# Three states of h instead of two, shorter rings for B and the scan inputs, and takes three slots behind the products

## The chip, the cores and the metric

The kernel runs on one core of one Trainium2 chip. The metric is the time of the slowest core in microseconds (us); with one core that is simply the time of the program on the device. The median of three runs before the change is 8832.22 us.

## The reference

The input x has 8192 rows of 512 numbers. The program computes x = x + layernorm(mamba(layernorm(x))) and then x = x + layernorm(soft mixture of experts(layernorm(x))). All of it is float32. The change lies in the mamba part, which has two layers and reads, cut to what matters:

```python
xc, z = split(x @ W_in.T)                 # 1024 channels each
u = silu(causal_conv4(xc) + b_c)
dt, B, C = split(u @ W_x.T)               # 32, 16 and 16 columns
delta = softplus(dt @ W_dt.T + b_dt)
h[t] = exp(delta[t] * A) * h[t-1] + delta[t] * B[t] * u[t]     # per channel and each of 16 states
y = sum over states of h * C + u * D
out = (y * silu(z)) @ W_out.T
```

The recurrence over t runs for 1024 channels times 16 states over 8192 rows, in each of two layers.

## The kernel before

**Tiling.** Each layer is cut into 16 chunks of T = 512 rows, so there are 32 chunks in all, numbered G. Channels lie on the 128 partitions, in NB = 8 blocks. A chunk has GROUPS = 32 groups, k = 0 to 31: one of the two halves of the blocks (HB = 4 blocks) with one of the 16 states. A group is four scans, one for each block of the half. So a chunk is SLOTS_BODY = 128 slots, slot s = 4k + b. All engines walk through the same 128 slots, each in an instruction stream that is written out in full, and semaphores tie them together.

**What each engine does in a slot.**

- ScalarE (ACT) computes the decay exp(delta * A) of the slot into PSUM (`decay_of`, L747). There are four such buffers, one bank each, so ACT runs at most four slots ahead of the scans.
- GpSimd (POOL) computes the inputs of two scans at once, w * B with w = delta * u, in one instruction for a pair of slots (`inputs`, L952). It reads a row of B repeated over all partitions (`b_rep`, loaded by SyncE, `load_b`, L404). `b_rep` has four rows and `bu` has four pairs. POOL also adds softplus parts, forms w, and adds pairs of products (`W_AT`, `SUM_AT`), 24 more instructions of the same size in a chunk.
- VectorE (DVE) runs the scan (`scan`, L1028) into `h[:, k % 2, b, :]`. After it DVE takes the transposed state of the group before, multiplies it by C and adds it up (`add_state`, L1048). Three of four such tiles fall to DVE and one to ACT (`product`, L763). In slots 4 and 5 of each eight no add falls to DVE.
- TensorE (PE) transposes the state of the group before, one tile j of 128 rows in each slot (`turn_states`, L538): tile (k-1, j) stands in slot 4k + j + 1, so tile (k-1, 3) stands in the first slot of group k+1. The transposes go to two PSUM banks in turn (`turn_bank`). Behind its tile PE does the slot's share of the projections (L467, L513), whose results go to a ring of two PSUM banks, `proj`. Skip tiles (u * D, L546, slots 4 to 7 and 30 to 39) and y tiles (L554, slots 22 to 28 and 116 to 122) come on top of the state tiles.

**The order of the projections** is written out by `timetable()`. It walks through `ORDER` (conv_half, conv, out, x_proj, turn_c, delta and gate tiles), gives each slot about equal PE work (`WORK`), and puts the moment when ACT takes a finished tile out of its bank TAKE_LAG = 4 slots behind the tile's last product (`TAKE`). A conv tile may start CONV_LAG slots behind its conv_half tile, and turn_c XDBL_LAG slots behind x_proj. The silu of u and of z runs over a whole half (128x2048) behind the last take of the half. It needs another table of functions than exp, so there is a table load ahead of it and one behind it. `silu_at` moves a silu further back when it would fall just ahead of ACT's products.

**The waits around the change.** A scan of the first slot of group k waits until tile (k-2, 3) has been transposed and until `h_last` of group k-2 has been saved, since it overwrites that state. `load_b` for group k waits until the inputs of group k-4 are made. `inputs` for slots s and s+1 waits until scan s-5 is done (`s - 6 + C_SCAN`).

Of the kernel before, what the change touches and what calls it, by code (L numbers as in the profile page):

```python
# [5 lines left out]
ALU = mybir.AluOpType  # L6
# [4 lines left out]
P = 128  # L11
# [7 lines left out]
T = 512  # L19
# [27 lines left out]
PRODUCTS = {"delta": 1, "conv_half": KD, "conv": TAPS, "out": NB, "x_proj": NB, "delta_next": 1, "turn_c": 1, "gate": KD}  # L47
SLOTS_BODY = GROUPS * HB
PAIRS = SLOTS_BODY // 2
TAKE_LAG, TAPS_LEAD, XDBL_LAG, CONV_LAG, PROD_LAG = 4, 2, 4, 4, 2  # L50

W_AT = {17: ("sum", 2), 21: ("product", 2), 25: ("sum", 3), 29: ("product", 3),
        49: ("sum_next", 0), 53: ("product_next", 0), 57: ("sum_next", 1), 61: ("product_next", 1)}
# [35 lines left out]
WEIGHT = {"x_proj": 1.1, "delta": 1.25, "delta_next": 1.25, "turn_c": 0.5, "state": 0.55, "skip": 1.05, "y": 0.55}  # L89

def silu_at(end):
    at = end + TAKE_LAG
    behind = (at - PROD_LAG - 5) % (2 * J)
    return at if behind < 5 else at + 2 * J - behind


def timetable():
    room = [-sum(WEIGHT[tile[0]] for tile in tiles_at) for tiles_at in TURN_AT]  # L100
    whole = sum(PRODUCTS[kind] * WEIGHT.get(kind, 1.0) for kind, _, _ in ORDER) - sum(room)
    room = [r + whole / (SLOTS_BODY - 3) for r in room]
    slot, left, end_of = 0, room[0], {}
    work, take = [[] for _ in range(SLOTS_BODY)], [[] for _ in range(2 * SLOTS_BODY)]
    for i, (kind, x, earliest) in enumerate(ORDER):
        if kind == "conv":
            earliest = end_of["conv_half", x] + CONV_LAG
        if kind == "x_proj":
            earliest = silu_at(end_of["conv", NB - 1]) + 1
# [12 lines left out]
        end = end_of[kind, x] = slots[-1]  # L122
        if kind == "conv_half":
            take[end + TAKE_LAG - TAPS_LEAD].append(("taps", x, i))
        take[end + TAKE_LAG].append((kind, x, i))
        if kind.startswith("delta") and x % 2 == 1:
            for q, part in enumerate(("exp", "ln")):
                take[end + TAKE_LAG + 1 + q].append((part + kind[5:], x // 2, i))
        if kind == "conv" and x % HB == HB - 1:
            take[silu_at(end)].append(("silu_u", x // HB, i))  # L130
        if kind == "gate" and x % HB == HB - 1:
            take[silu_at(end)].append(("silu_z", x // HB, i))
    return work, take, end_of


# [80 lines left out]
C_SCAN, C_HS, C_BU, C_XC, C_Z, C_Y, C_W, C_PROJ, C_TURN, C_PROD, C_DEC = 8, 2, PAIRS, NB, 2, NB, NB, 8, 8, 8, SLOTS_BODY  # L216


class Kind:
# [52 lines left out]
def mamba_stack(nc, ctx, d):  # L272
    def sb(name, shape):
        return ctx.enter_context(nc.sbuf_tensor(name, shape, F32))

    def ps(name, shape):
        return ctx.enter_context(nc.psum_tensor(name, shape, F32))

    def sem(name):
        return ctx.enter_context(nc.semaphore(name))  # L280
# [19 lines left out]
    xdbl = sb("xdbl", [P, T])  # L300
    c_next = sb("c_next", [P, J, STATES])
    c_now = sb("c_now", [P, J, STATES])
    b_rep = sb("b_rep", [P, 4, T])
    bu = sb("bu", [P, 4, 2, T])
    h = sb("h", [P, 2, HB, T])
    h_last = sb("h_last", [P, GROUPS * HB])
    prod = sb("prod", [P, 3, 2, HB * P])
    acc = sb("acc", [P, 2, J, HB * P])
    stage = sb("stage", [P, T])
    spare = sb("spare_m", [P, 1])  # L310

    decay = ps("decay", [P, HB, T])
    turn = ps("turn", [P, TURNS, T])
    proj = ps("proj", [P, RING, T])

# [6 lines left out]
    out_weights_in = sem("out_weights_in")  # L322
    xconv_in = sem("xconv_in")
    xgate_in = sem("xgate_in")
    brep_in = [sem(f"brep_in{r}") for r in range(4)]
    b_stored = sem("b_stored")
    out_stored = sem("out_stored")
    ident_set = sem("ident_set")
# [29 lines left out]
    def _(sp):  # L358
# [38 lines left out]

        def load_b(G, k):

            sp.wait_ge(bu_set, G * PAIRS + (2 * (k - 4) + 2 + C_BU))  # L400
            if k == 0:
                sp.wait_ge(b_stored, G * 16 + 32)
            src = d["b_rows"][bass.ds(G, 1), k % STATES, :].rearrange("a t -> (a t)").partition_broadcast(P)
            sp.dma_start(b_rep[:, k % 4, :], src).then_inc(brep_in[k % 4], 16)  # L404

        def body(G, kind, before_last=False):
            new = kind.layer + 1
# [52 lines left out]
    def _(pe):  # L460
# [72 lines left out]
        def turn_states(out, G, k, j):  # L533

            if j == 0:
                pe.wait_ge(scanned, G * SLOTS_BODY + (HB * k + HB + C_SCAN))
            for b in range(HB):
                mm = pe.transpose(out[:, b * P:(b + 1) * P], h[:, k % 2, b, j * P:(j + 1) * P], ident[:])  # L538
            mm.then_inc(turn_full, 1)

        def skip(out, G, layer, hf, j):
# [85 lines left out]
    def _(act):  # L627
# [113 lines left out]
        def decay_of(G, kind, k, b):  # L741
            hf, n = divmod(k, STATES)
            blk, s = hf * HB + b, HB * k + b
            act.wait_ge(scanned, G * SLOTS_BODY + (s + 1 - HB + C_SCAN))
            if n == 0:
                act.wait_ge(delta_set, G * HB + (blk // 2 + 1))
            act.activation(decay[:, b, :], delta[:, blk, :], ACT.Exp,  # L747
                           scale=neg_a[:, n, blk:blk + 1]).then_inc(decay_set, 1)

        def product(G, kind, tile):  # L750
# [26 lines left out]
        def save_last(G, k):  # L777

            act.wait_ge(scanned, G * SLOTS_BODY + (HB * k + HB + C_SCAN))
            act.copy(h_last[:, HB * k:HB * k + HB], h[:, k % 2, :, T - 1]).then_inc(hlast_set, 1)  # L780

        exp_tables()
        X, n = 0, 0
# [128 lines left out]
    def _(pool):  # L912
# [30 lines left out]
        def inputs(G, k, pr):  # L943

            hf, n = divmod(k, STATES)
            blk, s = hf * HB + 2 * pr, HB * k + 2 * pr
            if pr == 0:
                pool.wait_ge(brep_in[k % 4], G * (GROUPS * 4) + (k // 4 + 1) * 16)
# [3 lines left out]
            pool.tensor_tensor(bu[:, s // 2 % 4, :, :], w[:, blk:blk + 2, :],  # L952
                               b_rep[:, k % 4, :].unsqueeze(1).to_broadcast([P, 2, T]), ALU.mult).then_inc(bu_set, 1)

        def scaled(G, kind, tile, carried):
            turns, base = kind.turns, act_base(G, kind)
# [55 lines left out]
    def _(dve):  # L1012
# [4 lines left out]
        def scan(G, kind, k, b):  # L1017
            s = HB * k + b
            dve.wait_ge(decay_set, G * SLOTS_BODY + (s + 1))
            dve.wait_ge(bu_set, G * PAIRS + (s // 2 + 1 + C_BU))  # L1020
            if b == 0:

                dve.wait_ge(hlast_set, G * GROUPS + (k - 2 + 1 + C_HS))
                tile = "state", (k - 2) % GROUPS, J - 1
                if tile in kind.turns.index:
                    dve.wait_ge(turn_full, turn_base(G, kind) + (kind.turns.index[tile] + 1))
            start = zeros[:, 0:1] if kind.first or kind.enters else h_last[:, s:s + 1]
            dve.tensor_tensor_scan(h[:, k % 2, b, :], decay[:, b, :], bu[:, s // 2 % 4, b % 2, :], start,  # L1028
                                   ALU.mult, ALU.add).then_inc(scanned, 1)

        def add_state(G, kind, k, j):
# [890 lines left out]
```

## Time and profile before

| | |
|---|---|
| median of three runs | 8832.22 us (8822.1 to 8835.82) |
| the profiled execution's own time | 8832.35 us |
| span of its trace | 8829.7 us |
| mean granted TensorE clock | 0.928 |
| PE busy | 7621.7 us, 86% |
| DVE busy | 7550.2 us, 86% |
| POOL busy | 6729.4 us, 76% |
| ACT busy | 5909.6 us, 67% |

The scans run from 242 us to about 7970 us of the span. What is before is the input norm and the first chunk's projections, what is behind is the mixture of experts. The page's chain of work that ended last lies in the last stage only, so for the mamba stage one reads which wait ends last on the busiest engine. Matmul ends are modelled, so PE's busy time is not its limit by itself.

### The profile page before, as it was taken

The numbers are of one execution on the slowest core, as the hardware profiler recorded it, in microseconds if no ns is written. First come the engines' busy times: TensorE is split into PE (matmuls) and PEld (weight loads), VectorE is DVE, ScalarE is ACT, GpSimd is POOL, SyncE is SP. The second block draws the span as 40 slices with busy tenths as digits, with TensorE's granted clock in tenths as the row PEclk, the third lists the DMA queues.
The fourth block names the chain that finished last, engine by engine and source line by source line (L and its number), as shares of the span: only waits on it lengthen the run. The fifth ranks groups of instructions, "written<-read, shape, count | busy, mean of one in ns | idle before, by whom it ended". The sixth has DMA issues, their size and how long they took to land. (4 is left out here: it accounts for less than half of the span.)

```text
span 8829.7 us, 103475 instructions
## 1 busy us (share of the span) xinstructions
PE 7621.7 (86%) x31688; PEld 4308.0 (49%) x31688; DVE 7550.2 (86%) x8674; ACT 5909.6 (67%) x10830; POOL 6729.4 (76%) x2890
## 2 busy tenths in 40 slices
PE   5788888888889888888888888888888888876886
PEld 3444454444444444444444444444444444445753
DVE  2899999999999999999999999999999999995717
ACT  5777777677677777766777777777766776754515
POOL 0888888888888888888888888888888888881203
PEclk7899999999999999999999999999999999977789
DMA  5111111111111111121111111111111111113434
GB/s 192 49 50 48 44 48 50 49 50 50 50 46 50 48 50 44 48 60 59 60 50 50 44 52 50 50 48 44 48 50 50 50 50 50 41 43 136 176 117 152
DMA packets 223325, 550.37 MB, mean 62 GB/s; under 512 B 26272, under 2 KB 26528, under 8 KB 201824
## 3 DMA queue, kind: packets, MB, share of 16 engines
q1 hardware_dynamic: 196448, 459.30, 16.6%
q10 hardware_dynamic: 26368, 84.95, 2.4%
q8 instruction: 239, 3.92, 0.2%
q14 instruction: 270, 2.21, 0.1%
HBM read 442.44 MB, written 101.71 MB: 62 GB/s over the span
## 5 line engine op out<-in xcount | busy, mean ns | idle before, releaser
L952 POOL TENSOR_TENSOR bu<-w,b_rep 128x1024 f32<-128x1024 f32 x2048 | 4822.4, 2361 | 1160.1 <-DVE h L1028 1157.6
L1028 DVE TENSOR_TENSOR_SCAN h<-decay,h_last,bu 128x512 f32<-128x512 f32 x3840 | 4810.5, 1273 | 340.9 <-PE turn L538 271.5
L747 ACT ACTIVATE decay<-delta,neg_a 128x512 f32<-128x512 f32 x4096 | 2804.8, 690 | 1377.1 <-DVE h L1028 1309.7
L538 PEld LDWEIGHTS turn<-ident_m,h 128*128 128x128 f32 x16384 | 1997.2, 146 | 2987.5 <-DVE acc L1048 1582.8
L538 PE MATMUL turn<-ident_m,h 128*128 128x128 f32 x16384 | 2665.0, 288 | 635.3 <-DVE acc L1048 502.2
L1048 DVE SCALAR_TENSOR_TENSOR acc<-turn,c_now,acc 128x512 f32<-128x512 f32 x3072 | 2240.2, 729 | 190.6 <-PE turn L538 188.8
L763 ACT ACTIVATE prod<-turn,c_now 128x512 f32<-128x512 f32 x1024 | 701.6, 685 | 675.3 <-PE turn L538 674.5
L467 PE MATMUL proj<-zy,w_out 128*128 128x512 f32 x2048 | 1123.6, 654 | 19.9 <-ACT delta L714 19.0
L467 PE MATMUL proj<-conv_in,conv_diag 128*128 128x512 f32 x2048 | 1047.7, 608 | 71.0 <-ACT halo L681 71.0
L967 POOL TENSOR_TENSOR prod<-prod 128x1024 f32<-128x1024 f32 x448 | 1056.0, 2357 | 14.7 <-ACT prod L763 14.7
L467 PE MATMUL proj<-x_gate,w_in 128*128 128x512 f32 x2048 | 1054.1, 619 | 0.0
L467 PE MATMUL proj<-x_conv,w_in 128*128 128x512 f32 x2048 | 1018.8, 596 | 20.7 <-DMA x_conv<-xt 17.4
L467 PEld LDWEIGHTS proj<-zy,w_out 128*128 128x128 f32 x2048 | 371.5, 213 | 206.0 <-issue 169.4
L1028 DVE TENSOR_TENSOR_SCAN h<-decay,zeros_m,bu 128x512 f32<-128x512 f32 x256 | 320.1, 1272 | 145.2 <-POOL bu L952 123.1
L467 PEld LDWEIGHTS proj<-conv_in,conv_diag 128*128 128x128 f32 x2048 | 333.3, 194 | 217.3 <-issue 113.2
L467 PEld LDWEIGHTS proj<-x_gate,w_in 128*128 128x128 f32 x2048 | 347.2, 200 | 140.6 <-issue 140.6
L467 PEld LDWEIGHTS proj<-x_conv,w_in 128*128 128x128 f32 x2048 | 332.4, 191 | 166.1 <-issue 154.5
L934 POOL TENSOR_TENSOR delta<-delta,w 128x1024 f32<-128x1024 f32 x128 | 302.0, 2359 | 92.9 <-ACT w L722 92.9
L513 PE MATMUL proj<-xdbl,w_dt 65*128 65x512 f32 x512 | 297.3, 665 | 75.5 <-ACT stage L737 75.1
L546 PE MATMUL turn<-d_diag,u 128*128 128x128 f32 x2048 | 293.3, 287 | 67.2 <-DVE acc L1048 51.6
L673 ACT ACTIVATE conv_diag<-ident_m,par 128x128 f32<-128x128 f32 x1024 | 325.1, 392 | 3.6 <-DMA par<-in_par_dram 3.6
L546 PEld LDWEIGHTS turn<-d_diag,u 128*128 128x128 f32 x2048 | 251.9, 194 | 106.6 <-DVE acc L1048 73.2
(170 smaller groups left out, 5911.5 us busy)
## 6 DMA issues: line engine op xcount, KB each, us to landing
b_rep<-b_rows SPq DMA_DIRECT2D x1024, 256.0 KB, 3.2
x_conv<-xt SPq DMA_DIRECT2D x32, 1024.0 KB, 6.9
x_gate<-xt SPq DMA_DIRECT2D x32, 1024.0 KB, 4.8
xt<-stage ACTq DMA_DIRECT2D x128, 256.0 KB, 3.3
x_n<-in_x_dram SPq DMA_DIRECT2D x16, 1024.0 KB, 5.6
xt<-xt_n ACTq DMA_DIRECT2D x16, 1024.0 KB, 4.3
x_l<-in_x_dram SPq DMA_DIRECT2D x16, 1024.0 KB, 6.1
mt_l<-xt SPq DMA_DIRECT2D x16, 1024.0 KB, 6.1
```

The costliest lines, as they stand in the source:

```text
L467: mm = pe.matmul(out[0:lhs.shape[1], :], lhs, rhs, start=n == 0, stop=n == count - 1)
L513: pe.matmul(out, w_dt[:, b * P:(b + 1) * P], xdbl[0:XD + 1, :], start=True, stop=True).then_inc(proj_full, 1)
L538: mm = pe.transpose(out[:, b * P:(b + 1) * P], h[:, k % 2, b, j * P:(j + 1) * P], ident[:])
L546: mm = pe.matmul(out[:, b * P:(b + 1) * P], u[:, hf * HB + b, j * P:(j + 1) * P], d_diag[:, hf * HB + b, :], start=True, stop=True)
L673: act.activation(conv_diag[:, b % 2, k, :], ident[:], ACT.Copy, scale=par[:, STATES + k, b:b + 1])
L747: act.activation(decay[:, b, :], delta[:, blk, :], ACT.Exp, scale=neg_a[:, n, blk:blk + 1]).then_inc(decay_set, 1)
L763: act.activation(prod[:, V_BUFFER[q], k % 2, :], turn[:, BANK[tile], :], ACT.Copy, scale=c_now[:, j, n:n + 1]).then_inc(v_done, 1)
L934: pool.tensor_tensor(delta[:, lo:lo + 2, :], delta[:, lo:lo + 2, :], w[:, lo:lo + 2, :], ALU.add).then_inc(delta_set, 1)
L952: pool.tensor_tensor(bu[:, s // 2 % 4, :, :], w[:, blk:blk + 2, :], b_rep[:, k % 4, :].unsqueeze(1).to_broadcast([P, 2, T]), ALU.mult).the ...
L967: pool.tensor_tensor(total, total, prod[:, V_BUFFER[q]], ALU.add).then_inc(vsum_set, 1)
L1028: dve.tensor_tensor_scan(h[:, k % 2, b, :], decay[:, b, :], bu[:, s // 2 % 4, b % 2, :], start, ALU.mult, ALU.add).then_inc(scanned, 1)
L1048: dve.scalar_tensor_tensor(out, src, scalar, out, ALU.mult, ALU.add).then_inc(x_done, 1)
```

## The change

The state h gets three buffers, the rows of B two, the scan inputs three pairs. All the rings now run on over the chunks (group or slot number modulo the ring's length). The three lags of the timetable go from 4 to 3 and `silu_at` is dropped, so a silu follows the take of its last tile directly. The memory used stays the same: h grows by 8 KB in each partition, b_rep and bu shrink by 4 KB each. Worked out from the timetable, in slots: silu of u moves from 42 to 41 and from 65 to 64, silu of z from 119 to 114 and from 130 to 128 (that is slot 2 and slot 0 of the next chunk). The projections behind x_proj start one slot earlier (77 instead of 78), and their takes come two slots earlier in places: the take of the second out tile moves from slot 87 to 85, of the third from 95 to 93.

```diff
-TAKE_LAG, TAPS_LEAD, XDBL_LAG, CONV_LAG, PROD_LAG = 4, 2, 4, 4, 2
+TAKE_LAG, TAPS_LEAD, XDBL_LAG, CONV_LAG, PROD_LAG = 3, 2, 3, 3, 2
+H_RING = 3
+B_RING = 2
+DEC_RING = 4
+BU_RING = 3
-def silu_at(end):
-    at = end + TAKE_LAG
-    behind = (at - PROD_LAG - 5) % (2 * J)
-    return at if behind < 5 else at + 2 * J - behind
...
-            take[silu_at(end)].append(("silu_u", x // HB, i))
+            take[end + TAKE_LAG].append(("silu_u", x // HB, i))
...
-            take[silu_at(end)].append(("silu_z", x // HB, i))
+            take[end + TAKE_LAG].append(("silu_z", x // HB, i))
...
-    b_rep = sb("b_rep", [P, 4, T])
-    bu = sb("bu", [P, 4, 2, T])
-    h = sb("h", [P, 2, HB, T])
+    b_rep = sb("b_rep", [P, B_RING, T])
+    bu = sb("bu", [P, BU_RING, 2, T])
+    h = sb("h", [P, H_RING, HB, T])
...
-            sp.wait_ge(bu_set, G * PAIRS + (2 * (k - 4) + 2 + C_BU))
+            n = G * GROUPS + k
+            sp.wait_ge(bu_set, G * PAIRS + (2 * (k - B_RING) + 2 + C_BU))
...
-            pool.wait_ge(scanned, G * SLOTS_BODY + (s - 6 + C_SCAN))
+            pool.wait_ge(scanned, G * SLOTS_BODY + (s + 2 - 2 * BU_RING + C_SCAN))
...
-                dve.wait_ge(hlast_set, G * GROUPS + (k - 2 + 1 + C_HS))
-                tile = "state", (k - 2) % GROUPS, J - 1
-                if tile in kind.turns.index:
-                    dve.wait_ge(turn_full, turn_base(G, kind) + (kind.turns.index[tile] + 1))
+                dve.wait_ge(hlast_set, G * GROUPS + (k - H_RING + 1 + C_HS))
+                old = "state", (k - H_RING) % GROUPS, J - 1
+                if k >= H_RING or old in CARRIED and not kind.first:
+                    dve.wait_ge(turn_full, turn_base(G, kind) + (kind.turns.index[old] + 1))
+                elif not kind.first:
+                    dve.wait_ge(turn_full, turn_base(G, kind) + (ALL_TURNS.index[old] + 1 - TURN_TILES))
```

The other lines replace `k % 2`, `k % 4` and the like by the running numbers modulo the new lengths.

## Rows read from the trace of the kernel before

**Rows 1.** Timeline of SyncE's queue (start us, length us, what): loads of x_gate.

```profile
2179.17 0.33 SPq L391 DMA_DIRECT2D x_gate<-xt  x1
...
2421.52 0.33 SPq L391 DMA_DIRECT2D x_gate<-xt  x1
```

**Rows 2.** Waits of DVE, 200 to 8000 us: total us, times, longest.

```profile
DVE h L1028 <- PE turn L538: 287.8, 278, 3.1
DVE acc L1048 <- PE turn L538: 188.8, 189, 3.4
DVE zy L1057 <- ACT zy L731: 128.2, 32, 4.0
...
DVE h L1028 <- ACT decay L747: 73.6, 93, 1.3
```

**Rows 3.** Busy by stretch (PE, PEld, DVE, ACT, POOL; clock): tenth chunk, five stretches.

```profile
2419.40:2661.75 242.35, 215.76 (x900) 118.56 (x900) 220.41 (x233) 171.14 (x318) 205.46 (x89) 0.95 0.15 49
2465.36:2468.77 3.41, 3.41 (x8) 1.68 (x7) 2.68 (x3) 2.38 (x4) 3.41 (x2) 0.50 0.22 76
2557.51:2560.93 3.42, 3.09 (x13) 2.95 (x14) 3.42 (x4) 3.02 (x7) 3.42 (x2) 0.50 0.11 32
2574.58:2577.99 3.41, 3.41 (x8) 1.58 (x7) 2.73 (x3) 3.41 (x8) 2.15 (x1) 0.50 0.48 154
2591.65:2598.48 6.83, 6.20 (x12) 2.82 (x11) 2.85 (x4) 5.42 (x9) 6.35 (x3) 0.50 0.26 76
2639.43:2646.26 6.83, 5.75 (x16) 3.58 (x17) 5.29 (x6) 4.21 (x8) 4.46 (x2) 0.50 0.07 17
```

**Rows 4.** Timelines of PE and DVE, slots 85 to 96: idle time in brackets.

```profile
2573.83 1.37 PE L513 MATMUL proj<-xdbl,w_dt 65*128 65x512 f32 x2 [1.25 <-ACT stage L737]
...
2590.23 1.12 PE L513 MATMUL proj<-xdbl,w_dt 65*128 65x512 f32 x2 [1.25 <-ACT stage L737]
...
2576.09 0.75 DVE L1048 SCALAR_TENSOR_TENSOR acc<-turn,c_now,acc 128x512 f32<-128x512 f32 x1 [0.68 <-PE turn L538]
...
2579.45 0.75 DVE L1048 SCALAR_TENSOR_TENSOR acc<-turn,c_now,acc 128x512 f32<-128x512 f32 x1 [1.42 <-PE turn L538]
...
2595.40 0.75 DVE L1048 SCALAR_TENSOR_TENSOR acc<-turn,c_now,acc 128x512 f32<-128x512 f32 x1 [1.61 <-PE turn L538]
2599.26 1.28 DVE L1028 TENSOR_TENSOR_SCAN h<-decay,h_last,bu 128x512 f32<-128x512 f32 x1 [3.11 <-PE turn L538]
```

**Rows 5.** Timelines of ACT and DVE, slots 116 to 120: the silu of z.

```profile
2635.29 1.28 ACT L731 ACT_TABLE_LOAD   x1
2636.58 1.91 ACT L731 ACTIVATE zy<-zy 128x2048 f32<-128x2048 f32 x1
...
2638.59 0.69 DVE L1057 TENSOR_TENSOR zy<-turn,zy 128x512 f32<-128x512 f32 x1 [4.01 <-ACT zy L731]
...
2647.21 1.28 DVE L1028 TENSOR_TENSOR_SCAN h<-decay,h_last,bu 128x512 f32<-128x512 f32 x1 [2.48 <-PE turn L538]
```

**Rows 6.** Timelines of ACT and DVE, slots 40 to 43: first silu of u.

```profile
2492.04 0.71 ACT L747 ACTIVATE decay<-delta,neg_a 128x512 f32<-128x512 f32 x1
...
2500.65 1.30 ACT L747 ACTIVATE decay<-delta,neg_a 128x512 f32<-128x512 f32 x2
...
2494.49 1.28 DVE L1028 TENSOR_TENSOR_SCAN h<-decay,h_last,bu 128x512 f32<-128x512 f32 x1 [0.85 <-ACT decay L747]
...
2501.38 1.28 DVE L1028 TENSOR_TENSOR_SCAN h<-decay,h_last,bu 128x512 f32<-128x512 f32 x1 [1.29 <-ACT decay L747]
```

**Rows 7.** POOL from slot 97 on, DVE at slot 114, and b_rep's issues.

```profile
2602.53 2.36 POOL L952 TENSOR_TENSOR bu<-w,b_rep 128x1024 f32<-128x1024 f32 x1 [3.99 <-DVE h L1028]
...
2621.39 7.01 POOL L952 TENSOR_TENSOR bu<-w,b_rep 128x1024 f32<-128x1024 f32 x3
...
2629.64 1.28 DVE L1028 TENSOR_TENSOR_SCAN h<-decay,h_last,bu 128x512 f32<-128x512 f32 x1
...
DMA to landing us min/median/max: 3.0/3.2/10.0
```

More of the change, by code:

```diff
@@ L108, in timetable @@
         if kind == "x_proj":
-            earliest = silu_at(end_of["conv", NB - 1]) + 1
+            earliest = end_of["conv", NB - 1] + TAKE_LAG + 1
         if kind in ("turn_c", "delta_next"):
@@ L215 @@
 TURN_TILES, TURN_FIRST = len(ALL_TURNS.order), len(FIRST_TURNS.order)
-C_SCAN, C_HS, C_BU, C_XC, C_Z, C_Y, C_W, C_PROJ, C_TURN, C_PROD, C_DEC = 8, 2, PAIRS, NB, 2, NB, NB, 8, 8, 8, SLOTS_BODY
+C_SCAN, C_HS, C_BU, C_XC, C_Z, C_Y, C_W, C_PROJ, C_TURN, C_PROD, C_DEC = 8, H_RING, PAIRS, NB, 2, NB, NB, 8, 8, 8, SLOTS_BODY
 class Kind:
@@ L310, in mamba_stack @@
     spare = sb("spare_m", [P, 1])
-    decay = ps("decay", [P, HB, T])
+    decay = ps("decay", [P, DEC_RING, T])
     turn = ps("turn", [P, TURNS, T])
@@ L324, in mamba_stack @@
     xgate_in = sem("xgate_in")
-    brep_in = [sem(f"brep_in{r}") for r in range(4)]
+    brep_in = [sem(f"brep_in{r}") for r in range(B_RING)]
     b_stored = sem("b_stored")
@@ L403, in load_b @@
             src = d["b_rows"][bass.ds(G, 1), k % STATES, :].rearrange("a t -> (a t)").partition_broadcast(P)
[L404 removed]
+            sp.dma_start(b_rep[:, n % B_RING, :], src).then_inc(brep_in[n % B_RING], 16)
         def body(G, kind, before_last=False):
@@ L537, in turn_states @@
             for b in range(HB):
-                mm = pe.transpose(out[:, b * P:(b + 1) * P], h[:, k % 2, b, j * P:(j + 1) * P], ident[:])
+                mm = pe.transpose(out[:, b * P:(b + 1) * P], h[:, (G * GROUPS + k) % H_RING, b, j * P:(j + 1) * P], ident[:])
             mm.then_inc(turn_full, 1)
@@ L743, in decay_of @@
             blk, s = hf * HB + b, HB * k + b
-            act.wait_ge(scanned, G * SLOTS_BODY + (s + 1 - HB + C_SCAN))
+            act.wait_ge(scanned, G * SLOTS_BODY + (s + 1 - DEC_RING + C_SCAN))
             if n == 0:
                 act.wait_ge(delta_set, G * HB + (blk // 2 + 1))
-            act.activation(decay[:, b, :], delta[:, blk, :], ACT.Exp,
+            act.activation(decay[:, (G * SLOTS_BODY + s) % DEC_RING, :], delta[:, blk, :], ACT.Exp,
                            scale=neg_a[:, n, blk:blk + 1]).then_inc(decay_set, 1)
@@ L779, in save_last @@
             act.wait_ge(scanned, G * SLOTS_BODY + (HB * k + HB + C_SCAN))
-            act.copy(h_last[:, HB * k:HB * k + HB], h[:, k % 2, :, T - 1]).then_inc(hlast_set, 1)
+            act.copy(h_last[:, HB * k:HB * k + HB], h[:, (G * GROUPS + k) % H_RING, :, T - 1]).then_inc(hlast_set, 1)
         exp_tables()
@@ L945, in inputs @@
             hf, n = divmod(k, STATES)
-            blk, s = hf * HB + 2 * pr, HB * k + 2 * pr
+            blk, s, g = hf * HB + 2 * pr, HB * k + 2 * pr, G * GROUPS + k
             if pr == 0:
-                pool.wait_ge(brep_in[k % 4], G * (GROUPS * 4) + (k // 4 + 1) * 16)
+                pool.wait_ge(brep_in[g % B_RING], (g // B_RING + 1) * 16)
             if n == 0:
                 pool.wait_ge(w_set, G * NB + (blk + 2 + C_W))
-            pool.wait_ge(scanned, G * SLOTS_BODY + (s - 6 + C_SCAN))
-            pool.tensor_tensor(bu[:, s // 2 % 4, :, :], w[:, blk:blk + 2, :],
-                               b_rep[:, k % 4, :].unsqueeze(1).to_broadcast([P, 2, T]), ALU.mult).then_inc(bu_set, 1)
+            pool.wait_ge(scanned, G * SLOTS_BODY + (s + 2 - 2 * BU_RING + C_SCAN))
+            pool.tensor_tensor(bu[:, (G * PAIRS + s // 2) % BU_RING, :, :], w[:, blk:blk + 2, :],
+                               b_rep[:, g % B_RING, :].unsqueeze(1).to_broadcast([P, 2, T]), ALU.mult).then_inc(bu_set, 1)
         def scaled(G, kind, tile, carried):
@@ L1021, in scan @@
             if b == 0:
-                dve.wait_ge(hlast_set, G * GROUPS + (k - 2 + 1 + C_HS))
-                tile = "state", (k - 2) % GROUPS, J - 1
-                if tile in kind.turns.index:
-                    dve.wait_ge(turn_full, turn_base(G, kind) + (kind.turns.index[tile] + 1))
+                dve.wait_ge(hlast_set, G * GROUPS + (k - H_RING + 1 + C_HS))
[4 more added lines that the diff above has]
+                    dve.wait_ge(turn_full, turn_base(G, kind) + (ALL_TURNS.index[old] + 1 - TURN_TILES))
             start = zeros[:, 0:1] if kind.first or kind.enters else h_last[:, s:s + 1]
-            dve.tensor_tensor_scan(h[:, k % 2, b, :], decay[:, b, :], bu[:, s // 2 % 4, b % 2, :], start,
+            dve.tensor_tensor_scan(h[:, (G * GROUPS + k) % H_RING, b, :], decay[:, (G * SLOTS_BODY + s) % DEC_RING, :], bu[:, (G * PAIRS + s // 2) % BU_RING, b % 2, :], start,
                                    ALU.mult, ALU.add).then_inc(scanned, 1)
```

## The prediction

> **What bounds the kernel now.** I read first the page's busy shares: PE and DVE are level, so neither is plainly the bound and the mamba stage has to be read by its waits. Then the repeat: SyncE's load of x_gate comes at 2179.17 and again one chunk later at 2421.52 [rows 1], so a chunk takes 242.35 us, and nearly all chunks repeat it closely. In one chunk DVE works 220.41 us, PE 215.76, POOL 205.46, ACT 171.14 [rows 3]. DVE has the most work and stands idle for 21.9 us of 242.35. A stage in which DVE never waited would take 220.4 us a chunk; everything I can win lies in those 21.9 us. Over the stage DVE's waits [rows 2] are 287.8 (scan behind a transpose), 188.8 (add behind a transpose), 128.2 (gating behind the silu of z) and 73.6 (scan behind a decay): 678.4 us in all, 21.2 for each of 32 chunks. (POOL's wait for the first chunk's inputs is not counted, the change doesn't touch it.)
>
> The reader should then see where in the chunk these waits sit, since they are few and large, and that they have causes two steps back. In slots 85 and 92 PE stands 1.25 us because ACT has not yet taken an out tile out of the two-bank ring; right behind it DVE waits 0.68 and 1.42, and 1.61 and 3.11 [rows 4]. The granted clock shows why the second numbers are larger than 1.25: it is 0.50, that is 1.2 GHz, in 2574.58 to 2577.99 and in 2591.65 to 2598.48, just behind the two stands of PE, and 2.4 GHz between [rows 3]. At slot 116 DVE waits 4.01 us for the silu of z, PE stands with it, the clock is at 1.2 GHz from 2639.43 to 2646.26, and DVE waits another 2.48 at slot 120 [rows 3, 5]. So a late take or a late silu is paid twice, once as the wait and once as the slow clock behind it. Five stretches of 23.9 us together are at the low clock in each chunk, PE busy in 21.9 of them [rows 3]: at the high clock that work would be about 10.9 us shorter, PE's work then 204.8 us a chunk. PE has room in 229 us, but not much.
>
> **Three states of h.** The scan of a group's first slot no longer waits for the transpose that PE does in the same slot; the tile it now waits for lies four slots back. 287.8 / 32 = 9.0 us a chunk. Some of what the waits view gives to decay belongs here as well: at slot 40 the scan starts at 2494.49 after 0.85 us idle, but its decay, started at 2492.04, was done at 2492.75 [rows 6]; what it waited for was the transpose. What is late next: in groups with even k the add in the same slot needs that very tile, 1.2 us later (the scan's length less its overlap). All waits but the 3.11 and the 2.48 are shorter than that and go for good; those two would keep 1.9 and 1.3 if PE were as late as now. The save of h_last is also asked for one group earlier; it costs nothing.
>
> **Takes after three slots.** The take of the second out tile moves from ACT's slot 87 to 85 while the PE tile that needs the bank moves from 85 to 84, so it gains a slot (1.7 us) on it, more than the 1.25 us that PE stands; moreover it now precedes ACT's products of slots 86 and 87 instead of following them. The same holds at slot 92. So the two stands go, the low clock behind them too, and with them 0.68 + 1.42 + 1.61 of the add waits and what would be left of the 3.11 [rows 4]. The price: ACT takes a tile when PE has only just finished it and may have to wait there. ACT may do the take of slot s+3 when scan s-1 is done, and PE's work of slot s ends about when scan s starts, so the wait is under 1 us, while up to four decays are done ahead. I put nothing for it, bounds 0 and 1 us a chunk. CONV_LAG and XDBL_LAG only permit earlier starts.
>
> **The silus.** That of z moves from slot 119 to 114. ACT can begin it when scan 110 and its decay are done, and the table load and the silu take 1.28 + 1.91 [rows 5]; z is there two slots ahead of slot 116. 128.2 / 32 = 4.0 us a chunk go, and the 2.48 behind it. In the other direction works the first silu of u, now in slot 41 instead of 42. ACT works there without a pause; the chain of table load, silu and table load is 4.5 us (1.28 + 1.91 + 1.28) [rows 5]. Today decay 43 stands behind it, comes out at 2501.3 and costs 1.29 us [rows 6]. After the change decay 42 stands behind it: ready one decay (0.65) earlier, at about 2500.7, but wanted by DVE a slot earlier and, with the 0.85 at slot 40 gone, at about 2497.3. That is a wait of up to 3.4 us; What ACT loses ahead of it by waiting for PE's tiles may be used by the earlier takes; I set the lower bound at half, 1.7. I take 3.0, near the upper end, because DVE arrives faster too. PE stands for most of it, and the other four stands of that size were followed by the low clock, so I add 1.0 (0 to 1.7, since a stretch of 3.41 us at half speed costs 1.7). The silus at slots 64 and 128 end about when the decay behind them is wanted: 0.4 together (0 to 2).
>
> Two rules of the Trainium skill bear on this term. In the silu's rows [rows 5] the silu starts at 2636.58, 0.01 us behind the end of its table load, so a switch costs 1.28 us. The Trainium skill (ScalarE: Activation LUTs, "What ACT_TABLE_LOAD costs") puts a drain of about 1380 ns on top of about 1283 ns; with two switches around each silu the wait at slot 42 would by the page be some 2.8 us longer, 32 x 2.8 = 90 us in all. The trace shows the load but no drain, and the sum goes without it. The Trainium skill (TensorE: Matmul & The Clock Gate, "Part 1: The HAM clock gate") says that the clock is halved by default and that only activity releases it; this speaks against the change at slot 42, where PE will stand longer than now, and for it at slots 85, 92 and 116.
>
> **Shorter rings.** POOL may make the inputs of a pair when the scan two slots later than before is done: some 3.4 us less in hand (two slots of 220.41 / 128 = 1.72 [rows 3]; where every slot has an add it is a little more). From 2602.53 on [rows 7] POOL works at 2.36 us an instruction with hardly a pause, since in slots 98 to 122 it has six instructions for each four pairs (14.2 us) against eight slots of DVE's (8 x 1.72 = 13.8). At the narrowest point, slot 114, its result is there at 2621.39 + 2.36 = 2623.75, and the scan starts at 2629.64 [rows 7], 5.9 us later; 3.4 less leaves 2.5. Cost nothing, up to 1 us a chunk if DVE is faster there. The rows of B are now asked for when the group two back is done. They land 3.2 us after issue [rows 7] and POOL has two more pairs to make meanwhile, at least 4.7 us. SyncE's queue behind it: the x_gate and x_conv loads of 1 MB are issued between two rows, each with five or more POOL instructions of room behind, so nothing. At the change of layers whole weight matrices go through that queue, where the longest landing of 10.0 us [rows 7] lies; I put 10 us once, bounds 0 and 30.
>
> **The sum.** What remains for DVE in a chunk: of the add waits 188.8 / 32 - (0.68 + 1.42 + 1.61) = 2.2, at slots with skip or y tiles, which the change leaves as they are; at slot 42 3.0 and 1.0 behind it; 0.4 at the other silus; and 1.4 that I put for waits on PE that come back (0 to 4): even at the high clock PE's 204.8 us are 93% of DVE's 220.4, so that it makes up for a delay only slowly. Together 8.0 us against 21.2. 32 x 8.0 = 256; 678 - 256 = 422 us less, 10 more at the change of layers. The profiled execution has 8832.35 us (its span of 8829.7 and 2.7 around it), within 0.2 of the median 8832.22. 8832.35 - 422 + 10 = 8420 us, about 229 us a chunk. Its own range, with the bounds of the terms, is 8320 to 8490.
>
> **The rivals.**
>
> *The late tiles stay late* (chance 0.15). If PE is late at slots 96 and 120 for reasons of its own, the adds behind wait for the rest. Of the 21.2 go about 7.4 of the scan waits (each up to 1.2) and the 4.0 at z, and 1.2 come at slot 42: 10.2 x 32 = 326, 8506 us. For it: 3.11 is more than twice 1.25. Against it: the low clock explains the rest.
>
> *PE becomes the bound* (0.13). PE's idle time, 26.6 us a chunk, is then not slack that DVE causes but the price of two banks and their order, and stays. Only the low clock at three of the five places goes, 5 to 6 us: 5.7 x 32 = 182, 8650 us. For it: PE and DVE have nearly the same work. Against it: through long stretches DVE doesn't wait at all.
>
> *Nothing comes back as a wait* (0.10): the 2.2 alone remain, 678 - 70 = 608, 8224 us. Against it speaks the silu of u.
>
> *ACT's silus stop the decays* (0.06, slower). Without `silu_at` and with one slot less, each of the four silus comes when ACT's lead is used up, and DVE waits for the whole chain of 4.5 us and a take and decay behind it, about 5.7 us. Four times 5.7 and the 2.2 make 25 us a chunk against 21.2: 8832 + 122 = 8954 us. It decides from 4.8 us a silu on. Against it: ACT works 171 of 242 us [rows 3], and today DVE waits for decays only 73.6 / 32 = 2.3 us a chunk [rows 2], two silus of u and two of z included.
>
> *The change doesn't do what it says* (0.04): DVE and PE wait for each other by way of the two transpose banks, and each wait taken away comes back at the next add. Then it is 8832 within some us.
>
> **How the numbers follow.** Forecast 0.52, late tiles 0.15, PE 0.13, nothing comes back 0.10, silus 0.06, no effect 0.04. The first three hold 0.80 and reach from 8320 to 8650; with some room for the size of the first, 8290 to 8660. Faster by over 0.2%: 0.52 + 0.15 + 0.13 + 0.10 = 0.90; within 0.2%, about what a measurement of this kernel can tell from no change: 0.04; slower: 0.06.
>
> **What the profile after would show.** If each step is right: no scan in a group's first slot waits for a transpose; no wait of gating for the silu of z; PE's 1.25 us in front of delta tiles gone, and the low clock in three stretches a chunk instead of five; a single wait of about 3 us of a scan for its decay at slot 42; no scan that waits for POOL; x_gate loads 229 us apart. Wrong it would be if add waits grow by as much as scan waits fall, if scans wait for decays behind all four silus, or if POOL waits for B.

## The result and the profile after

The changed kernel takes 8279.26 us (median of four runs, 8267.94 to 8285.23) against 8827.16 us for the kernel before on the same chip. The ratio is 0.9377, with a 95% interval of 0.9361 to 0.9394. The forecast was 8420 us and its range began at 8290, so the direction was right, the time lies 11 us below the range, and the gain of 548 us was a third larger than the 412 that the sum gave. The mean granted clock of the profiled execution is 0.964, before it was 0.928.

The page after the change, busy time of each engine and the granted clock in 40 slices (compare the shares in the table of before, where DVE had 86%):

```profile
PE 7286.1 (88%) x31688; PEld 4150.8 (50%) x31688; DVE 7510.0 (91%) x8674; ACT 5880.2 (71%) x10830; POOL 6706.9 (81%) x2890
...
PEclk7899999999999999999999999999999999987789
```

DVE's waits from 200 to 7450 us, the mamba stage (total us, times, longest), to be set against [rows 2]:

```profile
DVE h L1029 <- POOL bu L951: 122.6, 1, 122.6
DVE h L1029 <- ACT decay L746: 100.6, 93, 3.2
DVE acc L1049 <- PE turn L537: 67.2, 114, 2.5
DVE zy L1058 <- PE turn L553: 7.5, 3, 7.0
```

Two of the four large entries are gone: the scan never waits for a transpose any more (287.8 before), and gating never for the silu of z (128.2). The add's waits fell from 188.8 to 67.2. Only the waits for a decay grew, from 73.6 to 100.6. The entry for POOL is the first chunk's and stood before the change too (124.6).

Busy time by stretch, in the columns of [rows 3]: the tenth chunk, and the twenty-sixth, which is in the second layer:

```profile
2253.10:2476.68 223.58, 203.74 (x900) 112.68 (x900) 219.04 (x233) 170.21 (x318) 204.68 (x89) 1.00 0.17 53
5847.80:6072.97 225.17, 205.42 (x900) 113.22 (x900) 219.13 (x234) 170.19 (x318) 204.73 (x89) 0.99 0.19 52
```

A chunk takes 223.58 us instead of 242.35. DVE works 219.04 of it, so 4.54 us are left in which it stands. The granted clock is 1.00 over the whole chunk, where it was 0.95 before with five stretches at 0.50. In the twenty-sixth chunk there is one such stretch again, at slots 76 to 78 (the chunk's mean is 0.99), and that chunk is 1.6 us longer with the same instructions. Of the first 31 chunks (no scan of a next one marks the end of the last) 20 have no low stretch at all, the eighteenth to the twenty-sixth have this one, and only the first chunk and the seventeenth, where the layers change, have more.

### The profile page after: what moved, and what is told of

It is laid out like the page before. It is cut to its first block and busy times, and to the rows that moved or that the text cites. A ratio compares the mean times of both kernels' runs of the same rounds, so it can differ in the third digit from the quotient of the medians.

```text
span 8272.7 us, 103474 instructions
## 1 busy us (share of the span) xinstructions
PE 7286.1 (88%) x31688; PEld 4150.8 (50%) x31688; DVE 7510.0 (91%) x8674; ACT 5880.2 (71%) x10830; POOL 6706.9 (81%) x2890
## 5 line engine op out<-in xcount | busy, mean ns | idle before, releaser
L537 PEld LDWEIGHTS turn<-ident_m,h 128*128 128x128 f32 x16384 | 1936.3, 142 | 2836.1 <-DVE acc L1049 1622.6
L537 PE MATMUL turn<-ident_m,h 128*128 128x128 f32 x16384 | 2569.9, 281 | 527.1 <-DVE acc L1049 498.9
L1049 DVE SCALAR_TENSOR_TENSOR acc<-turn,c_now,acc 128x512 f32<-128x512 f32 x3072 | 2234.4, 727 | 67.4 <-PE turn L537 67.2
L466 PE MATMUL proj<-conv_in,conv_diag 128*128 128x512 f32 x2048 | 1022.4, 595 | 18.5 <-ACT halo L680 18.5
L466 PE MATMUL proj<-zy,w_out 128*128 128x512 f32 x2048 | 1028.5, 604 | 0.9 <-DVE zy L1058 0.9
L466 PE MATMUL proj<-x_gate,w_in 128*128 128x512 f32 x2048 | 1023.5, 594 | 0.0
L466 PEld LDWEIGHTS proj<-zy,w_out 128*128 128x128 f32 x2048 | 336.5, 194 | 149.0 <-issue 139.6
L466 PEld LDWEIGHTS proj<-x_gate,w_in 128*128 128x128 f32 x2048 | 322.4, 191 | 77.0 <-issue 77.0
L940 POOL TENSOR_TENSOR w<-delta,u 128x1024 f32<-128x1024 f32 x128 | 303.4, 2370 | 0.3
```

Source lines behind the costliest of these rows:

```text
L466: mm = pe.matmul(out[0:lhs.shape[1], :], lhs, rhs, start=n == 0, stop=n == count - 1)
L537: mm = pe.transpose(out[:, b * P:(b + 1) * P], h[:, (G * GROUPS + k) % H_RING, b, j * P:(j + 1) * P], ident[:])
L940: pool.tensor_tensor(w[:, lo:lo + 2, :], delta[:, lo:lo + 2, :], u[:, lo:lo + 2, :], ALU.mult).then_inc(w_set, 2)
L1049: dve.scalar_tensor_tensor(out, src, scalar, out, ALU.mult, ALU.add).then_inc(x_done, 1)
```

## The experiments

Four questions were open. Which half of the change does what? Are late takes and late silus really paid twice? Why is so little left over? What do the shorter rings cost? Theory A is that of the prediction: a stand of PE costs itself and then the slow clock behind it. Against it stood that the third state of h takes up all of PE's lateness (B), or just what PE loses to the clock (C).

**The rings alone.** The changed kernel with the lags and `silu_at` of before (the lines of `silu_at` are left out here):

```diff
-TAKE_LAG, TAPS_LEAD, XDBL_LAG, CONV_LAG, PROD_LAG = 3, 2, 3, 3, 2
+TAKE_LAG, TAPS_LEAD, XDBL_LAG, CONV_LAG, PROD_LAG = 4, 2, 4, 4, 2
```

> The new rings (three states of h, two rows of B, three pairs of scan inputs) with the old lags of four slots and the old places of the silus. Theory A, a late take is paid twice: PE still stands in front of the delta tiles and at the silu of z, so its clock is still at 1.2 GHz for some 20 us of a chunk. The 9 to 10 us a chunk of scans that wait for a transpose go, but about 3 us come back as add waits and the 4.0 us for the silu of z stay: about 14 us of waits a chunk, 8610 us, between 8550 and 8660. Theory B, the third state of h takes up PE's lateness altogether: under 8450 us with add waits under 3 us a chunk.

Measured: 8577.33 us, ratio 0.9722 (0.9706 to 0.9738). DVE's waits over the stage:

```profile
DVE acc L1055 <- PE turn L543: 233.2, 269, 2.8
DVE zy L1064 <- ACT zy L736: 142.1, 32, 4.8
...
DVE h L1035 <- ACT decay L752: 70.4, 32, 2.2
```

The busy times of its tenth chunk:

```profile
2343.46:2577.49 234.03, 210.12 (x900) 117.55 (x900) 219.87 (x233) 170.66 (x318) 205.10 (x89) 0.96 0.16 50
```

As theory A has it. No scan waits for a transpose, but the adds wait more than before (233.2 us against 188.8, that is 1.4 us a chunk where I expected about 3), the waits for the silu of z are 142.1 us against 128.2, and PE's clock is down for 13.7 to 17.1 us of nearly every chunk. The new rings alone give 246 us of the 548.

**The lags alone.** The kernel before with one line changed:

```diff
-TAKE_LAG, TAPS_LEAD, XDBL_LAG, CONV_LAG, PROD_LAG = 4, 2, 4, 4, 2
+TAKE_LAG, TAPS_LEAD, XDBL_LAG, CONV_LAG, PROD_LAG = 3, 2, 3, 3, 2
```

> The kernel before with lags of three slots; two states of h, four rows of B, four pairs of scan inputs. Theory A: PE no longer stands for ACT, its clock stays at 2.4 GHz in nearly the whole stage (at most one low stretch a chunk), and the scan waits that remain are the short ones at slots with skip and y tiles, 3 to 4 us a chunk; with 4.5 us of other waits about 8 us a chunk, 8410 us, between 8370 and 8460. Theory B: without the third state the lateness of PE stays, above 8600 us.

Measured: 8317.33 us, ratio 0.9428 (0.9412 to 0.9443), 53 us below the lower end of what theory A gave. DVE's waits over the stage:

```profile
DVE h L1028 <- PE turn L538: 84.8, 133, 1.2
DVE h L1028 <- ACT decay L747: 63.6, 93, 3.2
DVE acc L1048 <- PE turn L538: 46.5, 71, 2.1
```

Its tenth chunk by busy time:

```profile
2271.50:2496.76 225.26, 204.30 (x900) 112.51 (x900) 219.43 (x234) 170.71 (x318) 205.23 (x89) 1.00 0.16 52
```

The lags bring 506 of the 548 us. Of the 287.8 us of scan waits, for which the third state of h was meant, 203 go without it. Most of these are the 3.11 us at slot 96 and the 2.48 us at slot 120 [rows 4, 5], which stood behind PE's stands and its slow clock: 5.6 us a chunk, 179 in all. The two parts overlap: alone they give 246 and 506, together 548. The three lags were only shifted together; what CONV_LAG and XDBL_LAG do by themselves is not shown.

**Two states of h with everything else as changed.**

```diff
-H_RING = 3
+H_RING = 2
```

> The changed kernel with two states of h again; lags of three slots, two rows of B and three pairs of scan inputs stay. If the shorter rings of B and of scan inputs cost nothing, this agrees with the kernel that has the lags alone within 10 us, and no scan waits for POOL after the first chunk. If they cost, it is slower than that one by more than 20 us, with waits of scans for POOL or of POOL for the rows of B.

Measured: 8348.33 us, ratio 0.946 (0.9444 to 0.9476). That is 31 us slower than the lags alone on the same chip, which differ from it only in the longer rings of B and of scan inputs. So the rings do cost, though no scan waits for POOL. ACT's waits show by what way; this line is absent in the kernel with the lags alone:

```profile
ACT prod L762 <- POOL prod L966: 108.7, 94, 2.0
```

POOL has less in hand, so its sum of two products comes later, ACT may overwrite the buffer later, and the second silu of u behind ACT's product starts later: the wait for decay 65 is 0.48 us against 0.14. That is 0.35 us a chunk (225.60 against 225.25 where the clock stays up), some 11 us in all. (That the 0.35 comes by this way is read from the rows, not isolated.) The rest lies mostly in nine chunks like the first of these two neighbours, which have 6.8 us at the low clock and take 2.4 to 2.6 us more; with the lags alone just two chunks have a low stretch, beside the first and the one where the layers change:

```profile
2275.47:2503.67 228.20, 207.63 (x900) 114.44 (x900) 219.64 (x234) 170.54 (x318) 204.94 (x89) 0.99 0.15 52
2503.67:2729.26 225.59, 204.31 (x900) 112.53 (x900) 219.42 (x233) 170.64 (x318) 204.78 (x89) 1.00 0.17 52
```

The changed kernel has that last line too, with 105.7 us: it comes with the rings, not with the two states. Against two states the third is worth 69 us, 2.2 a chunk, with 84.4 us of scan waits taken away. Part of these come back: the wait at slot 42 is 1.54 us with two states and 2.48 with three.

**Late takes.** The changed kernel; only ACT's takes of the later out tiles and of the next deltas, with the exp and ln of these deltas, come one slot later, the takes four behind their products:

```diff
+        late = 1 if kind == "delta_next" or kind == "out" and x > 0 else 0
-        take[end + TAKE_LAG].append((kind, x, i))
+        take[end + TAKE_LAG + late].append((kind, x, i))
...
-                take[end + TAKE_LAG + 1 + q].append((part + kind[5:], x // 2, i))
+                take[end + TAKE_LAG + late + 1 + q].append((part + kind[5:], x // 2, i))
```

> The changed kernel, but ACT takes the out tiles from the second on and the delta tiles of the next chunk four slots behind their last product again; PE's order is untouched. Theory A: PE stands about 1 us in front of the second and fourth delta tile, the clock falls to 1.2 GHz behind it, and DVE waits 3.5 to 4.8 us more a chunk around slots 86 to 96: 8390 to 8430 us. Theory B: three states of h take the lateness up, no low clock or no cost of it, under 8310 us.

Measured: 8524.98 us, ratio 0.9662 (0.9646 to 0.9678): 246 us slower than the changed kernel, nearly half of the whole gain lost by one slot of seven tiles. PE's and then DVE's timeline in its tenth chunk, where the clock is low only for 3.4 us, at slot 94:

```profile
2481.73 1.13 PE L513 MATMUL proj<-xdbl,w_dt 65*128 65x512 f32 x2 [1.25 <-ACT stage L737]
2485.04 1.98 PE L467 MATMUL proj<-zy,w_out 128*128 128x512 f32 x4 [1.75 <-ACT delta L714]
...
2487.50 0.75 DVE L1050 SCALAR_TENSOR_TENSOR acc<-turn,c_now,acc 128x512 f32<-128x512 f32 x1 [2.37 <-PE turn L538]
2503.83 0.75 DVE L1050 SCALAR_TENSOR_TENSOR acc<-turn,c_now,acc 128x512 f32<-128x512 f32 x1 [2.87 <-PE turn L538]
```

Two neighbouring chunks by busy time:

```profile
2333.10:2562.47 229.37, 204.97 (x900) 114.06 (x900) 219.34 (x234) 170.35 (x318) 204.93 (x89) 0.99 0.17 51
2562.47:2797.31 234.84, 210.51 (x900) 116.63 (x900) 219.55 (x233) 170.45 (x318) 204.88 (x89) 0.96 0.16 50
```

Both terms of theory A are there and can nearly be told apart. With the clock nearly always up (229.37) the late takes cost 5.8 us a chunk against 223.58: PE stands twice 1.25 and twice 1.75 us. In the neighbour the same instructions have 13.7 us more at 1.2 GHz, PE's busy time is 5.54 us longer, and the chunk takes 5.47 us more. But the slow clock does not follow each stand: ten of the 31 chunks are like the first of these two, with the stands and without the low clock behind slot 86. The size was underrated: 8390 to 8430 us were expected, 3.5 to 4.8 us a chunk more.

**The silu of z late.** The changed kernel with the silu of z at slots 119 and 130 again.

```diff
-            take[end + TAKE_LAG].append(("silu_z", x // HB, i))
+            take[end + TAKE_LAG + (5 if x < HB else 2)].append(("silu_z", x // HB, i))
```

> The changed kernel with the silu of z put back to slots 119 and 130, takes and rings as changed. Theory A, a wait in which PE stands is paid twice: DVE waits 4 to 4.5 us at slot 116 for the silu, PE's clock is at 1.2 GHz behind it in most chunks, and 1.5 to 2.5 us of add waits follow at slots 118 to 120: 6 to 7 us a chunk, 8470 to 8500 us. Theory C, the third state of h takes up what PE loses to the clock: only the 4 to 4.5 us themselves, 8405 to 8425 us.

Measured: 8446.08 us, ratio 0.9572 (0.9558 to 0.9587): 167 us more than the changed kernel, 5.2 a chunk, between the two theories. DVE's timeline at slot 116:

```profile
2515.70 0.69 DVE L1058 TENSOR_TENSOR zy<-turn,zy 128x512 f32<-128x512 f32 x1 [4.99 <-ACT zy L730]
```

That chunk and the next by busy time:

```profile
2307.89:2536.28 228.39, 205.18 (x900) 113.20 (x900) 219.04 (x233) 170.82 (x318) 204.88 (x89) 0.99 0.17 52
2536.28:2766.22 229.94, 206.98 (x900) 114.84 (x900) 219.16 (x233) 170.72 (x318) 204.88 (x89) 0.99 0.17 51
```

The wait itself is 4.99 us, longer than I gave. Behind it the clock falls, but in the first of these chunks no further wait follows; its 4.8 us over 223.58 are the wait alone. Here theory C is right: with three states the 2.48 us at slot 120 [rows 5] don't come back. 4.8 us a chunk are 154 of the 167 us. The rest does come by the clock, but elsewhere: the second of these chunks has a further stretch from slot 76 on, and the add at slot 78 waits 1.45 us. So with three states a late silu of z is paid once.

**Only two pairs of scan inputs.**

```diff
-BU_RING = 3
+BU_RING = 2
```

> The changed kernel with two pairs of scan inputs instead of three. POOL has two slots (3.4 us) less in hand again. The leads read after the change are 1.1 to 8.4 us, under 3.4 in some twelve pairs of 64 and least at slot 114; where they turn negative DVE waits for POOL. If POOL's lead is what the length of this ring buys, there are waits of scans for POOL in every chunk, 10 to 30 us of them, 8600 to 9250 us. If the lead is set by something else, under 8350 us.

Measured: 8901.03 us, ratio 1.0087 (1.0068 to 1.0105), 622 us slower than with three pairs and 74 us slower than the kernel before. DVE's waits over the stage:

```profile
DVE h L1029 <- ACT decay L746: 296.7, 137, 3.9
DVE h L1029 <- POOL bu L951: 242.6, 172, 122.9
DVE acc L1049 <- PE turn L537: 209.0, 417, 2.3
```

The total held, the way was not the expected one. Of the 242.6 us of waits for POOL 122.9 are the first chunk's, which were there before; some 120 are left, under 4 us a chunk. The larger part comes back elsewhere: waits for decays are up from 100.6 to 296.7 us and waits for transposes from 67.2 to 209.0. The way is the one seen with two states of h, twelve times as wide. ACT's largest wait is now for POOL's sum of two products, 1256.1 us against 105.7 after the change:

```profile
ACT prod L762 <- POOL prod L966: 1256.1, 432, 4.0
```

These rows fit one reading: with two pairs POOL gives out inputs only when the scans have nearly used them up, its other work comes late, ACT stands with its decays behind it, and DVE waits for these. (No run isolates these steps.) The length of this ring alone, three or two pairs, decides whether the changed kernel is the faster or the slower one: a margin of one pair.

**ACT's order before the silu of u.** The largest wait left is 2.48 us at slot 42. The changed kernel with exp and ln of the last deltas behind the first silu of u, and the second silu of u one slot later:

```diff
+            back = 5 if kind == "delta" and x == NB - 1 else 0
-                take[end + TAKE_LAG + 1 + q].append((part + kind[5:], x // 2, i))
+                take[end + TAKE_LAG + 1 + q + back].append((part + kind[5:], x // 2, i))
-            take[end + TAKE_LAG].append(("silu_u", x // HB, i))
+            take[end + TAKE_LAG + (1 if x == NB - 1 else 0)].append(("silu_u", x // HB, i))
```

> The changed kernel with two shifts in ACT's order: exp and ln of the last pair of deltas five slots later (43 and 44, behind the first silu of u instead of ahead of it), the second silu of u one slot later (65). If the waits at slots 42 (2.48 us) and 65 (0.47) come from what stands ahead of the silu on ACT, 2.1 us of work less ahead of decay 42 leaves at most 0.4 us there and nothing at 65: 2.4 to 2.8 us a chunk less, 8190 to 8205 us. If the work behind the silu catches the decays of slots 43 to 46 instead, or POOL's sum of that pair comes late, the gain comes back as waits there: 8260 us or more.

Measured: 8284.9 us, ratio 0.9387 (0.9375 to 0.94), no gain over the changed kernel. My expectation missed, and ACT's timeline says why:

```profile
2328.02 0.59 ACT L770 COPY acc<-turn 128x512 f32<-128x512 f32 x1 [1.71 <-PE turn L546]
2328.50 0.69 ACT L689 ACTIVATE u<-proj,par 128x512 f32<-128x512 f32 x1
2329.21 1.28 ACT L693 ACT_TABLE_LOAD   x1
```

The 2.1 us of work are gone from ahead of the silu, but now ACT stands 1.71 us for the skip tile of slot 39, which PE can only make when DVE is there. The wait at slot 42 is 2.37 us. The wait at slot 65 went as expected, but 16 of the first 31 chunks have a stretch at the low clock at slot 76 that costs them 1.6 us, where the changed kernel has it in nine.

**The skip tile moved**, alone and with the former shifts:

```diff
-SKIP_AT = ((7, 4, 5, 6), (30, 33, 36, 39))
+SKIP_AT = ((7, 4, 5, 6), (30, 33, 36, 44))
```

> The changed kernel with the last skip tile of the second half in slot 44 instead of 39 (the timetable spreads the projections around it again). In the kernel with exp and ln behind the silu, ACT stood 1.71 us for the transposed skip tile of slot 39 just ahead of the silu of u, so two things hold the silu: ACT's own work (exp and ln of the last deltas) and PE's skip tile, which comes only when DVE is at slot 39. If so, moving the skip tile alone frees only what the work leaves, about 0.5 us of the 2.48 at slot 42: 8255 to 8270 us. If the skip tile is the whole cause, 2 us or more a chunk: 8200 to 8215 us.

> Both shifts at once: the last skip tile in slot 44 and exp and ln of the last deltas in slots 43 and 44, the second silu of u in slot 65. If the two of them hold the silu together, the wait at slot 42 falls from 2.48 to at most 0.5 us and the one at slot 65 goes: 2.4 us a chunk less, 8190 to 8210 us. If there is a third thing ahead of it, or if ACT's products of slots 46 and 47 come late behind exp and ln, 8250 us or more.

Measured: alone 8304.01 us, ratio 0.9408 (0.9395 to 0.9421); with both shifts 8255.57 us, ratio 0.9355 (0.9342 to 0.9367). DVE's timeline of the kernel with both, slots 42 to 46:

```profile
2322.59 1.28 DVE L1030 TENSOR_TENSOR_SCAN h<-decay,h_last,bu 128x512 f32<-128x512 f32 x1 [0.56 <-ACT decay L747]
2328.35 2.46 DVE L1030 TENSOR_TENSOR_SCAN h<-decay,h_last,bu 128x512 f32<-128x512 f32 x2 [0.82 <-ACT decay L747]
2331.97 0.75 DVE L1050 SCALAR_TENSOR_TENSOR acc<-turn,c_now,acc 128x512 f32<-128x512 f32 x1 [1.16 <-PE turn L538]
```

The two causes do hold the silu together: alone the moved tile takes 0.5 us from the wait at slot 42 (1.98 left), with both it is 0.56. But 0.82 and 1.16 us come back right behind, and alone even 1.98 us at slot 46, where PE is late behind the moved tile at the low clock. That stretch is there in 28 of the first 31 chunks and costs 1.7 us in each; where it is missing the wait is 0.31 us. This made the kernel with the tile alone slower than the changed one, which I had not expected. The pair is 24 us below the changed kernel by the medians. These come from two chips, and the intervals of the two ratios (0.9342 to 0.9367 and 0.9361 to 0.9394) still touch, but the chunks at the high clock bear it out, with 0.7 us less than 223.58:

```profile
2470.36:2693.24 222.88, 203.38 (x900) 112.87 (x900) 219.15 (x234) 170.20 (x318) 204.71 (x89) 1.00 0.17 53
```

**ln one slot later, the skip tile in slot 45.** Against the kernel with both shifts:

```diff
-SKIP_AT = ((7, 4, 5, 6), (30, 33, 36, 44))
+SKIP_AT = ((7, 4, 5, 6), (30, 33, 36, 45))
-                take[end + TAKE_LAG + 1 + q + back].append((part + kind[5:], x // 2, i))
+                take[end + TAKE_LAG + 1 + q + back + (q if back else 0)].append((part + kind[5:], x // 2, i))
```

> As the kernel with both shifts, but the last skip tile in slot 45 and ln of the last deltas in slot 45 instead of 44. There 0.82 us at slot 45 (decay, behind exp, ln and the conv_half take) and 1.16 at slot 46 (PE late behind the skip tile at 1.2 GHz) came back. If it is ln that holds decay 45, the 0.82 goes and most of the 1.16 with it: 0.8 to 1.5 us a chunk less than there, 8210 to 8230 us. If the place just behind the silu is full whatever the order, 8250 us or more.

Measured: 8253.37 us, ratio 0.935 (0.9337 to 0.9362), the same as the former. The 0.82 is down to 0.25, but adds at slots 46 to 48 wait 1.29, 0.62 and 0.57 for PE. The room behind the silu is full in the orders tried.

## Why the prediction was right in its kind and short in its size

*What bounds the kernel.* Right: DVE bounds it, and the waits were few, large and had causes two steps back. DVE now works 98% of a chunk.

*Three states of h.* The scan waits went entirely. But most of them were not this part's to win: 203 of the 287.8 us go with the lags alone. Reading a wait's label as a part's worth would have misled; the sum did not suffer from it only because it was made over both parts.

*Takes after three slots.* Right in kind: PE's 1.25 us in front of the delta tiles are gone, and undoing this shift for seven tiles costs 246 us. The zero that I put for ACT waiting on PE holds too: DVE's six waits in the tenth chunk are at slots 1, 6, 14, 38, 42 and 65, none behind such a take.

*The silu of z.* Right: 4.0 us a chunk gone, and the 2.48 behind it.

*The silu of u.* Right in place and near in size. I put 3.0 us at slot 42; this is the scan, with 2.48:

```profile
2330.55 1.28 DVE L1029 TENSOR_TENSOR_SCAN h<-decay,h_last,bu 128x512 f32<-128x512 f32 x1 [2.48 <-ACT decay L746]
```

The other silus cost 0.67 (0.20 at slot 1, 0.47 at slot 65) where I put 0.4. The first table load starts at 2325.30 and takes 1.28, and the silu starts at 2326.60; the second starts at 2328.53 and takes 1.28, and the decay starts at 2329.82. The drain of some 1380 ns that the Trainium skill (ScalarE: Activation LUTs, "What ACT_TABLE_LOAD costs") gives for each switch did not show, and the measurement decides.

*What failed: the terms for waits on PE.* The mechanism held, but the sum left too much behind. I kept 0.97 at slot 26 inside the 2.2 of add waits, put 1.0 for the low clock behind slot 42, and 1.4 for waits on PE that come back because PE makes up for a delay only slowly. In the tenth chunk the 0.97 and the 1.0 are 0, and of the 1.4 only 0.25 at slot 14 came: add waits are 0.84 + 0.25 + 0.30 = 1.39. With 2.48 at slot 42 and 0.67 at the other silus that is 4.54 us measured where 8.0 were forecast. No row stood behind the 1.4.

The first two terms came from the three stretches at the low clock that I left in a chunk (at slots 25 and 75 and a new one behind slot 42); 20 of the first 31 chunks have none. I had argued that a stand of PE is followed by the low clock, since all five stretches were. That is not so. These are PE's stands at slot 24 to 25 before the change, and 0.9 us behind the second the clock fell:

```profile
2462.64 0.66 PE L554 MATMUL turn<-ident_m,acc 128*128 128x128 f32 x4 [0.48 <-DVE acc L1048]
2464.48 0.66 PE L538 MATMUL turn<-ident_m,h 128*128 128x128 f32 x4 [1.18 <-DVE acc L1048]
```

and these after it, where it did not:

```profile
2295.51 0.66 PE L553 MATMUL turn<-ident_m,acc 128*128 128x128 f32 x4 [0.48 <-DVE acc L1049]
2297.35 0.66 PE L537 MATMUL turn<-ident_m,h 128*128 128x128 f32 x4 [1.18 <-DVE acc L1049]
```

The stands agree to 0.01 us. Even PE's 1.80 us behind slot 42 was not followed by the low clock. The trace of before held the same answer, had I read more than the tenth chunk: its twentieth chunk has the same two stands, no low stretch behind them, and 239.19 us instead of 242.35.

```profile
4838.31:5077.50 239.19, 211.25 (x900) 115.65 (x900) 220.20 (x233) 171.06 (x318) 205.40 (x89) 0.97 0.16 49
4881.00:4890.00 9.00, 6.33 (x31) 3.78 (x31) 9.00 (x11) 5.47 (x13) 9.00 (x4) 1.00 0.09 29
...
4881.54 0.66 PE L554 MATMUL turn<-ident_m,acc 128*128 128x128 f32 x4 [0.48 <-DVE acc L1048]
4883.38 0.66 PE L538 MATMUL turn<-ident_m,h 128*128 128x128 f32 x4 [1.18 <-DVE acc L1048]
```

The Trainium skill (TensorE: Matmul & The Clock Gate, "Part 1: The HAM clock gate") has the throttled clock as the default state, which activity releases. The direction agrees: with the stands for ACT gone the mean granted clock rose from 0.928 to 0.964. Which single stand is followed by the low clock, no run here shows.

*A smaller term that was missing.* DVE's own busy time fell from 220.41 to 219.04 us a chunk, 44 us in all. I had taken 220.4 as fixed. An instruction that follows without a wait overlaps the one before by 0.08 to 0.09 us, as these of the kernel before, and is 0.01 to 0.02 us shorter; there are now 6 waits in a chunk instead of 19:

```profile
2463.70 0.73 DVE L1048 SCALAR_TENSOR_TENSOR acc<-turn,c_now,acc 128x512 f32<-128x512 f32 x1
2464.34 0.68 DVE L1057 TENSOR_TENSOR zy<-turn,zy 128x512 f32<-128x512 f32 x1
2464.93 1.27 DVE L1028 TENSOR_TENSOR_SCAN h<-decay,h_last,bu 128x512 f32<-128x512 f32 x1
```

*The rings.* I put nothing, up to 1 us a chunk. No scan waits for POOL, and the rows of B land in time (all 1024 loads, from issue to landing):

```profile
DMA to landing us min/median/max: 2.9/3.2/6.0
```

But the shorter rings are not free: 0.35 us a chunk by way of ACT's product buffers, a path I had not followed, and a further 20 us or so that goes with the low clock in some chunks. For the change of layers I put 10 us; the seventeenth chunk, where it lies, takes 228.28 us, 4.7 more than its neighbour at the high clock, and 3.0 of these are a longer wait for a decay at slot 1.

*The account.* The profiled execution took 8274.51 us, 145.5 under the forecast. Of the 678.4 us of waits 167.8 are left (100.6 for decays and 67.2 of the adds), so 511 went where I had 422 less the 10 for the change of layers: 99 more. DVE's busy time gives the other 44. Some 3 us remain outside these views.

*The range.* I gave 8320 to 8490 as the forecast's own range "with the bounds of the terms", but did not add the bounds up. With every term at its lower bound 2.2 and 1.7 us are left in a chunk, 125 in all, and the sum gives 8279 us, the measured median. That the two meet so closely is luck: 5.2 us of waits a chunk were left in the mean, 1.3 more than these 3.9, and DVE's busy time, which no bound covered, fell by as much. But a range that began there would have held the measured time. The 8290 is the 8320 with a little room; the case "nothing comes back" (8224 us, chance 0.10) was left outside, and what happened lies between it and the forecast.

## What to carry to other kernels

When several engines walk in step, find for each large wait the stand of another engine ahead of it, and sum the parts together, since two parts that remove the same wait can't be added: here 246 and 506 us make 548. Before a wait on a full queue is tuned, list everything in that queue ahead of it that itself waits for someone: taking away 2.1 us of work ahead of the silu gave nothing until the tile behind it was moved as well. A ring that is shortened may cost nothing at its own consumer and still cost elsewhere, so follow each later step of the engine that has less in hand.

## What the runs showed of the hardware

The same instructions ran at 2.4 GHz in one chunk and partly at 1.2 GHz in the next: 13.7 us more at the low clock lengthened a chunk by 5.47 us (229.37 and 234.84) with the takes late, one stretch of 3.41 us by 1.6 us after the change (223.58 and 225.17). The same two stands of PE, 0.48 and 1.18 us, were followed by the low clock in one chunk and not in another of the same kernel. A low stretch costs only where DVE then waits: the 3.41 us behind the late silu of z cost nothing (228.39 us, 4.8 over 223.58, with a wait of 4.99 for the silu). A VectorE instruction that starts without a wait saves about 0.1 us against one that has waited (1.37 us a chunk for 13 waits fewer).
